# Attention block with a distance effect: reciprocal softmax totals spread through DRAM by two ACT transfers in place of two TensorE products

## What is computed

```
scores = where(allow, scores * total_effect, NEG)
attn   = softmax(scores)                      # exp(..) / total
out    = einsum('bhqk,bhkd->bhqd', attn, v)
concat = out.transpose(0, 2, 1, 3).reshape(B, S, D)
query2 = concat @ Wo.T + bo
```

## Time and profile before

| what | value |
|---|---|
| median of 3 runs | 1515.24 us (1514.38 to 1515.81) |
| profiled execution, own time | 1516.79 us |
| its span | 1515.0 us |
| PE, DVE, ACT busy | 96%, 75%, 69% |
| granted TensorE clock, mean | 0.988 |

### The profile page before, as it was taken

How to read it: one execution, slowest core, us unless ns; L and a number is a source line. 1 busy time by engine, 2 the same in 40 slices (tenths; PEclk the granted TensorE clock), 3 DMA queues, 4 the chain that set the end, 5 groups by cost and what they waited for, 6 DMA issues and landing times.

```text
span 1515.0 us, 34684 instructions
## 1 busy us (share of the span) xinstructions
PE 1458.3 (96%) x13024; PEld 1221.1 (81%) x13024; DVE 1135.2 (75%) x3972; ACT 1044.6 (69%) x2690; POOL 80.9 (5%) x75
## 2 busy tenths in 40 slices
PE   5788799999999999999999999999999999999997
PEld 4456688888888888888888888888888888888886
DVE  6997778887887768687777877768787776868533
ACT  4765668687786767777676867768777677776622
POOL 4113000000000000000000000000000000000000
PEclk9899999999999999999999999999999999999999
DMA  7675656666566555655565555556565655564876
GB/s 279 248 251 197 223 195 254 234 223 237 198 258 226 211 206 213 209 200 209 212 232 207 211 207 209 206 203 233 207 224 190 225 215 203 215 209 171 331 278 250
DMA packets 64998, 337.27 MB, mean 223 GB/s; under 512 B 8384, under 2 KB 9408, under 8 KB 32192
## 3 DMA queue, kind: packets, MB, share of 16 engines
q1 hardware_dynamic: 64256, 335.06, 61.4%
q10 hardware_dynamic: 576, 0.00, 0.0%
HBM read 307.77 MB, written 27.26 MB: 221 GB/s over the span
## 4 chain that ended last, share of the span: by engine, by line
PE 86%; DVE 8%; DMA 2%; ACT 1%; issue 1%; POOL 0%; SPq 0%; POOLq 0%; ACTq 0%; DVEq 0%
PE bank L227 23%; PE bank L229 22%; PE bank L228 22%; PE bank L487 9%; PE bank L501 6%; PE bank L526 2%; DVE w_sb L1334 2%; DVE w_sb L1322 1%; PE bank L543 1%; DVE w_ring L1302 1%; PE bank L516 1%; DMA w_ring<-w_split 1%; PE bank L529 1%; DVE w_sb L1344 1%; DVE s_sb L1310 1%
## 5 line engine op out<-in xcount | busy, mean ns | idle before, releaser
L227 PE MATMUL bank<-xt_hi,w_ring 128*128 128x256 f32 x1024 | 298.5, 292 | 4.0 <-DMA w_ring<-w_split 2.2
L229 PE MATMUL bank<-xt_hi,w_ring 128*128 128x256 f32 x1024 | 290.2, 283 | 0.0
L228 PE MATMUL bank<-xt_lo,w_ring 128*128 128x256 f32 x1024 | 290.1, 283 | 0.0
L1310 DVE CUSTOM_DVE_ANT_0 s_sb<-bank,mask 128x256 f32<-128x256 f32 (+7 forms) x512 | 130.8, 304 | 150.6 <-PE bank L487 149.4
L920 ACT COPY pt_sb<-bank 128x512 f32<-128x512 f32 x192 | 111.5, 581 | 167.2 <-PE bank L501 167.2
L910 ACT ACTIVATE p_sb<-w_sb,nm 128x32 f32<-128x32 f32 (+7 forms) x512 | 205.7, 405 | 4.0 <-DVE nm L1349 3.9
L890 ACT ACTIVATE w_sb<-s_sb,nm 128x161 f32<-128x161 f32 (+7 forms) x512 | 164.2, 404 | 62.7 <-DVE nm L1318 62.7
L227 PE MATMUL bank<-w_ring,h_hi 128*128 128x512 f32 x512 | 206.7, 404 | 0.7 <-DMA w_ring<-w_split 0.7
L227 PEld LDWEIGHTS bank<-xt_hi,w_ring 128*128 128x128 f32 x1024 | 196.4, 192 | 11.7 <-issue 11.2
L229 PE MATMUL bank<-w_ring,h_lo 128*128 128x512 f32 x512 | 200.3, 391 | 0.0
L228 PE MATMUL bank<-w_ring,h_hi 128*128 128x512 f32 x512 | 200.1, 391 | 0.0
(11 more groups left out here) (136 smaller groups left out, 2928.9 us busy)
## 6 DMA issues: line engine op xcount, KB each, us to landing
w_ring<-w_split SPq DMA_DIRECT2D x252, 1024.0 KB, 4.9
w_split<-w_ring SPq DMA_DIRECT2D x32, 512.0 KB, 5.1
x_raw<-x_t SPq DMA_DIRECT2D x16, 512.0 KB, 3.8
c_raw<-ctx_t SPq DMA_DIRECT2D x16, 512.0 KB, 4.9
u_sb<-x_rows SPq DMA_DIRECT2D x16, 512.0 KB, 6.0
ring_raw<-w SPq DMA_DIRECT2D x32, 256.0 KB, 5.1
out<-rows SPq DMA_DIRECT2D x15, 512.0 KB, 7.1
ahead_c<-ctx_t SPq DMA_DIRECT2D x4, 512.0 KB, 8.9
```

Source lines behind the costliest of these rows:

```text
L227: nc.tensor.matmul(dst, a_hi, b_hi, start=start, stop=False)
L228: nc.tensor.matmul(dst, a_hi, b_lo, start=False, stop=False)
L229: return nc.tensor.matmul(dst, a_lo, b_hi, start=False, stop=stop)
L1310: m = nc.vector.tensor_tensor_reduce(out=s_sb[:, c % 2, W_AT[b] + 1:W_AT[b] + 1 + WIDTH[b]], in0=s_bank[n % 2][:, at:at + WIDTH[b]], in1=m ...
```

## The change

Both products, the split of the reciprocals, `zi_wide`, the matrix of ones and ACT's copy go. ACT's queue instead issues two transfers for each (batch, c): `zi_store` writes z2 (4 KB, 128 partitions of 32 bytes) to DRAM, and `zi_load` reads it back with each head's 1 KB repeated for its 32 partitions (128 KB arrive). `zi_load` waits for the store to have landed. `concat` waits for the load and for the product, and reads the reciprocals with a step of 8 elements. Core of the diff:

```
+    zi_out = nc.dram_tensor("zi_out", (NQ, P, NB), F32, kind="Internal").ap()
+        zi_row = tensor("zi_row", [P, 2, R * NB])
...
@@ attend
-                pe.wait_ge(wide_ok, NQ * i + c + 1)
-
-                for part in range(2):
-                    nc.tensor.matmul(av_bank[:, S:2 * S], head_ones_r[:], zi_wide[:, part].rearrange("p b r -> p (b r)"),
-                                     start=part == 0, stop=part == 1, skip_group_check=True)
...
-            def reciprocals(i, c):
-                act.wait_ge(av_mm, NQ * i + c + 1)
+            def zi_store(i, c):
+                act.wait_ge(zi2_ok, NQ * i + c + 1)
+                act.dma_start(zi_out[c], z2[:, c]).then_inc(zi_st, 16)
+
+            def zi_load(i, c):
+                act.wait_ge(zi_st, 16 * (NQ * i + c + 1))
                 if c >= 2 or i > 0:
-                    act.wait_ge(cc_lo_ok, NQ * i + c - 1)
-                nc.scalar.copy(cc_sb[:, c % 2], av_bank[:, S:2 * S]).then_inc(zi_row_ok, 1)
+                    act.wait_ge(cc_ok, NQ * i + c - 1)
+                act.dma_start(zi_row[:, c % 2], zi_out[c].rearrange("(h r) b -> h (r b)", h=HQ).unsqueeze(1)
+                              .broadcast_to([HQ, R, R * NB])).then_inc(zi_in[c % 2], 16)
...
@@ step, second quarter, ACT
                 if last:
                     turned(i - 1, 3, 0)
+                    zi_store(i - 1, 3)
                 if now:
                     effect(i, 0)
+                if last:
+                    zi_load(i - 1, 3)
                 if ffn:
                     features(i - 2, 4)
...
@@ final, ACT
                 turned(last, 3, 0)
+                zi_store(last, 3)
                 turned(last, 3, 1)
+                zi_load(last, 3)
                 features(ffn, 5)
...
@@ totals and concat, DVE
                 nc.vector.reciprocal(z2[:, c], z2[:, c]).then_inc(zi2_ok, 1)
-                dve.wait_ge(zi2_ok, 3 * (NQ * i + c) + 1)
-                nc.vector.tensor_copy(zi_pair[:, 0], z2[:, c]).then_inc(zi2_ok, 1)
-                dve.wait_ge(zi2_ok, 3 * (NQ * i + c) + 2)
-                nc.vector.tensor_tensor(zi_pair[:, 1], z2[:, c], zi_pair[:, 0].bitcast(F32),
-                                        ALU.subtract).then_inc(zi2_ok, 1)
...
-                dve.wait_ge(zi_row_ok, NQ * i + c + 1)
-                nc.vector.tensor_tensor(cc_sb[:, c % 2], av_bank[:, 0:S], cc_sb[:, c % 2], ALU.mult).then_inc(cc_ok, 1)
+                dve.wait_ge(av_mm, NQ * i + c + 1)
+                dve.wait_ge(zi_in[c % 2], 16 * ZI_LOADS * ((NQ * i + c) // 2 + 1))
+                nc.vector.tensor_tensor(cc_sb[:, c % 2].rearrange("p (b r) -> p b r", r=R),
+                                        av_bank[:, 0:S].rearrange("p (b r) -> p b r", r=R),
+                                        zi_row[:, c % 2].rearrange("p (r b) -> p b r", b=NB), ALU.mult).then_inc(cc_ok, 1)
```

More of the change, by code:

```diff
@@ L53, in build @@
     NP = FT // 2
+    ZI_LOADS = 1
     w1_split = nc.dram_tensor("w1_split", (NP, P, 2, 2 * 512), F32, kind="Internal").ap()
@@ L180, in build @@
         zi2_ok = sem("zi2_ok")
-        wide_ok = sem("wide_ok")
-        zi_row_ok = sem("zi_row_ok")
+        zi_st = sem("zi_st")
+        zi_in = [sem(f"zi_in{n}") for n in range(2)]
         cc_ok = sem("cc_ok")
@@ L1016, in first @@
                 turned(0, 0, 0)
+                zi_store(0, 0)
                 first_exp(0, 2)
+                zi_load(0, 0)
                 turned(0, 0, 1)
@@ L1030, in first @@
                 first_exp(0, 3)
+                zi_load(0, 1)
                 turned(0, 1, 1)
@@ L1043, in first @@
                 first_exp(1, 0)
+                zi_load(0, 2)
                 turned(0, 2, 1)
@@ L1056, in first @@
                 first_exp(1, 1)
+                zi_load(0, 3)
                 turned(0, 3, 1)
@@ L1068, in first @@
                 turned(1, 0, 0)
+                zi_store(1, 0)
                 first_exp(1, 2)
+                zi_load(1, 0)
                 ahead_copy(3, 1)
@@ L1082, in first @@
                 second_exp(1, 1, 1)
-                reciprocals(1, 0)
                 features(0, 0)
@@ L1087, in first @@
                 turned(1, 1, 0)
+                zi_store(1, 1)
                 concat_high(1, 0)
@@ L1090, in first @@
                 first_exp(1, 3)
+                zi_load(1, 1)
                 turned(1, 1, 1)
@@ L1102, in step @@
                     turned(i - 1, 2, 0)
+                    zi_store(i - 1, 2)
                     effect(i - 1, 3)
+                    zi_load(i - 1, 2)
                 if ffn:
@@ L1152, in step @@
                     turned(i, 0, 0)
+                    zi_store(i, 0)
                     effect(i, 1)
+                    zi_load(i, 0)
                 if ffn:
@@ L1175, in step @@
                     turned(i, 1, 0)
+                    zi_store(i, 1)
                     concat_high(i, 0)
                     effect(i, 2)
+                    zi_load(i, 1)
                 if last:
@@ L1211, in final @@
                 turned(last, 2, 0)
+                zi_store(last, 2)
                 effect(last, 3)
+                zi_load(last, 2)
                 turned(last, 2, 1)
@@ L1217, in final @@
                 second_exp(last, 3, 1)
-                reciprocals(last, 2)
                 deviation2(B - 3)
@@ L1686, in inputs_high @@
                 nc.gpsimd.tensor_copy(c_hi[:], c_raw[:]).then_inc(xc_hi_ok, 1)
-            for t, value in ((mask, 0.0), (ident, 0.0), (delta, 0.0), (head_ones, 0.0), (tiny, R_TINY), (eps, EPS_LN),
-                             (carry, 1.0), (p_sb, 0.0)):
+            for t, value in ((mask, 0.0), (ident, 0.0), (tiny, R_TINY), (eps, EPS_LN), (carry, 1.0), (p_sb, 0.0)):
                 then(nc.gpsimd.memset(t[:], value))
@@ L1706, in _ @@
             assert made[0] == DISTS
-            for h in range(HQ):
-                on = slice(R * h, R * h + R)
-                then(nc.gpsimd.affine_select(out=delta[on], in_=delta[on], compare_op=ALU.not_equal, fill=1.0,
-                                             base=0, pattern=[[-1, R]], channel_multiplier=1))
-                then(nc.gpsimd.memset(head_ones[on, on], 1.0))
             then(nc.gpsimd.affine_select(out=ident[:], in_=ident[:], compare_op=ALU.not_equal, fill=1.0, base=0,
                                          pattern=[[-1, P]], channel_multiplier=1))
-            then(nc.gpsimd.tensor_copy(head_ones_r[:], head_ones[:]))
             assert made[0] == CONSTS
@@ L1758, in _ @@
             over_batches(first, step, final)
-MASKS = 8 + 4
+MASKS = 6 + 4
 STARTS = MASKS + 4
 DISTS = STARTS + 4 + 1
-CONSTS = DISTS + 8 + 1 + 1
+CONSTS = DISTS + 1
 COLS = 3
```

25 lines of the change are left out of this document (3 added, 22 removed).

## The result

The changed kernel takes 1528.28 us (median of 4 runs, 1526.90 to 1530.66) against 1515.31 us for the kernel before beside it: ratio 1.0086, interval [1.0073, 1.0099]. The prediction was 1496.2 us. It is wrong by 32 us, and in its sign. The profiled execution has a span of 1525.5 us, 10.5 more than before.

A forecast was written before the change was run, and what follows sets the result against it. DVE was taken to bound the start (to about 160 us), PE the rest. 14.2 + 6.3 - 1.5 = 19.0 us less, median 1515.24 to 1496.2 us; forecast 1492 to 1500 us (0.53), range 1491 to 1511 us.

The forecast's parts named there:

- PE's products: Two products of each attend on PE, 0.24 us together; 59 attends on the chain give 14.2 us less.
- DVE's split and widening: In the start, where DVE rules: 1.05 us saved six times in the chain, 6.3 us less; nothing in the steady part.
- the start gives nothing: Rival, chance 0.12: split weights' stores and loads, or a GpSimd copy, pace the start; 1502.5 us.
- The multiplication: DVE's `concat` with one input at a step of 8 elements takes its 0.42 us again: no cost.
- The issues on ACT: Two issues for each (batch, c), 0.9 us on ACT, hide beside the instructions dispatched before them: cost 0.
- The wait for the store: In ACT's queue the store lands 3.8 us after issue, under the 4.4 us limit: no PE wait in the steady part.
- the store lands a little late: Rival, chance 0.14: store lands at 4.7 us, 0.3 us x 28 quarters = 8.4 us come back; 1504.6 us.
- `final`: End of the program, ACT tight: 0.5 us for load's issue or short wait, 1.0 us for the load; 1.5 us cost.
- the load lands late: Rival, chance 0.04: DVE stands at `concat`; above 8.9 us excess paid at most 14 times; at 12 us, 1539 us.
- The load in the steady part: Issued at 723.0, wanted at 731.89, room 8.9 us against a highest row of 8.1 us: in time, cost 0.

The follow-up runs named there:

- run 1: Changed kernel without the store, the load and the waits for them, the row of reciprocals filled with ones once: 1499.81 us, 0.9888 of the kernel before.
- run 8: Kernel of run 7 with `turn_rows` moved behind the first scores of the step's last quarter on PE: 1501.82 us, 0.9911 of the kernel before.
- run 11: Kernel of run 1 with `zi_row` read contiguously by the concat, not in steps of eight elements: 1499.58 us, 0.9894 of the kernel before.
- run 7: Changed kernel with the edits of run 3 and run 4, plus the store of a step's last quarter behind `concat_high`: 1503.58 us, 0.9920.
- run 2: Kernel before, all its products, copies and splits kept, with store, load and DVE's wait for the load added: 1531.85 us, 1.0099.
- run 3: Changed kernel with the load moved behind the second copy of pt_sb in each step's first two quarters, one place later in `final`: 1516.72 us, 1.0002.
- run 4: Changed kernel with only the last two loads split by head into four transfers each: 1518.84 us, 1.0016 of the kernel before.
- run 5: Changed kernel with its last two loads cut into two transfers each, of two heads: 1524.82 us, 1.0067 of the kernel before.
- run 10: Changed kernel with store and load on GpSimd's queue, last two loads by head, `turn_rows` behind the last quarter's first scores: 1499.56 us, 0.9890.

## Why the prediction was wrong

- **"PE's products"** held as a size: 0.241 us for each of 56 in the steady part, where 0.24 was predicted. What it left out is that the 0.24 us were also cover. `turn_rows` comes right behind `attend`, and waits 0.24 us for a relu as soon as the products are gone: 3.3 us of the gain go back without any transfer (runs 1 and 8).
- **"DVE's split and widening"** held: the start is 6.2 us shorter, where 6.3 was predicted, and 6.1 to 7.7 in the other runs without the products (9.8 once). It is a net figure, with the products of five attends and a few waits for transfers in it. The rival that the start gives nothing is refuted.
- **"The multiplication"** was mis-sized (0.67 us, not 0.42), without effect on the time (run 11).
- **"The issues on ACT"**, "Hidden: 0", failed. It looked at two places, and in both `zi2_ok` comes long before the copy. In the fourth quarter it comes with the copy's end, the issue is exposed, and 3.4 us arrive at PE (run 7). The step counted an issue as hidden by its length alone; in these traces it is hidden where its wait is over while another instruction still runs. PE pays for it only because the two products are gone as well: with them in place (run 2) the small waits for x_lo don't come.
- **"The wait for the store"** failed, and it was the step that the text itself called the decisive one. The limit of 4.4 us was right within 0.2, and so was the 3.8 us as a typical time: it is the median of the steady part. What failed is that one value was compared with the limit ("That is under 4.4, so I take no wait"). Behind the weights' 1 MB the stores take 2.9 to 5.0 us, a third of them more than the limit, and each of these costs PE not the excess but 0.6 to 1.05 us. PE pays 8.3 us, nearly all in ten places. The rival *the store lands a little late* had a price of 8.4 us from 0.3 us in 28 quarters; that the numbers agree is luck, its path is right, and run 3 shows it.
- **"`final`"** failed by the most: 1.5 us predicted (0.5 and 1.0), 13.6 measured, 1.2 of them ahead of the end of `hidden(6)` and 12.4 behind it, 9.4 of these as one wait of PE. The store was to take 3.8 us and took 6.5; the load was to take up to 8.1 us and took 13.4 to its last piece. The reason was named beside the rival *the load lands late*, that the load uses four DMA engines, but was priced at a fraction (2.5 us), because the pieces' queueing behind 8 KB pieces was not worked out. Runs 4 and 5 show that shorter transfers alone don't help and four by head do. That the number of DMA engines is the cause fits the rates of the pieces, but the profile names no engine, so it isn't shown. Of the other 3.0 us, the slow clock is 1.4: the first seven products of `project_rows` begin 0.43 us apart, where products of that shape begin 0.23 apart in the steady part. Another 1.5 are a second spell of the slow clock, shown below.
- **"The load in the steady part"** held: DVE waits for `zi_row` only twice, both in `final`.

The second spell of the slow clock lies in this stretch of the changed kernel (PEclk 0.87 on the mean):

```profile
1480.00:1490.00 10.00, 10.00 (x62) 9.38 (x61) 2.10 (x5) 2.11 (x5) 0.00 (x0) 0.87 0.79 314
```

After a wait of 1.92 us for SP's weights, 16 products from 1479.08 on begin 0.21 us apart, where they begin 0.12 apart before the change. The kernel before has the same wait (1.9 us) and keeps its clock at 1.00 there. Run 1 has the spell without any transfer and run 11 doesn't have it, so these 1.5 us are not the transfers'.

Of the 32 us between forecast and result, `final` is 12.1 (13.6 where 1.5 was predicted; 1.5 of it the second spell of the slow clock), the late store in the steps 8.3, the issue 3.4, the lost cover 3.3, small pieces 1.6 and products of `final` that were counted but not gained 0.7. That makes 29.4 in the span; the medians differ by 2.5 more, since the run profiled before stood 1.55 above its median and the one after 1.0 below its own.

## What to carry to other kernels

A small transfer that an engine must wait for is priced by what else the DMA engines are moving when it is issued and by what stands behind the wait in that engine's queue. Compare the spread of its landing with the room, not its typical time. Where nothing that the bounding engine needs stands behind the wait, the same lateness costs next to nothing, be it by another place in the queue or by an idle engine's queue: as made, this change costs 0.9%; with other places on ACT's own queue and the last loads cut by head it gains 0.9% (run 8), on GpSimd's queue 1.1% (run 10). And when work is taken from the engine that bounds the kernel, look at which wait its length had covered before counting it as gained.

## What the runs showed of the hardware

- A store of 4 KB (128 pieces of 32 bytes) issued where the other queue moves less starts 0.8 us after its issue, is done at 1.0 at the earliest and lands at 1.4; issued behind 1 MB of another queue it starts after 1.9 to 2.75 us and the load that waits for it is issued after 2.9 to 5.0, in `final` after 6.5.
- A load with four entries in its outermost dimension had 106 of its 128 pieces through in 2 us and the last 22 in 7.4, one in 0.34 us, beside 8 KB pieces of 0.309 us. The same load took 13.5 us at an even 8 to 14 pieces in a us in run 3, and 7.1 us in run 2.
- GpSimd takes 0.56 us to issue the store and 0.70 us for the load, ACT 0.32 and 0.53.
- A VectorE product of 128x256 float32 takes 0.67 us with one input at a step of 8 elements and 0.42 us with all contiguous (run 11).
- After PE had waited 1.9 us for weights the granted clock fell to 0.50 for 3.4 us in two traces (changed kernel, run 1) and stayed at 1.00 in two others (kernel before, run 11).
